# Routed mixture stage: where its rows are scaled, how its front half is ordered, and how lanes are compared

## The reference, cut to what matters

```
logits = x @ gate_w                      # 2048 x 8
top_val, top_id = max(logits), argmax(logits)
score = sigmoid(top_val)
xs = x * score
y[e] = (silu(xs @ rt_gate[e]) * (xs @ rt_up[e])) @ rt_down[e]
routed = y[top_id]                       # one expert for each token
shared = (silu(x @ sh_gate) * (x @ sh_up)) @ sh_down
return shared + routed
```

## Time and profile before

| | |
|---|---|
| median of 3 runs | 928.35 us |
| the profiled execution | 928.58 us, its span 926.8 us |
| mean granted TensorE clock | 0.923 |
| PE, DVE, ACT, POOL busy | 81%, 73%, 40%, 42% |
| first mixture stage | starts near 446.7 us |
| second mixture stage | starts near 812.7 us |
| 23 gathers (L1551), both stages | 43.7 us on POOL |

### The profile page before, as it was taken

How to read it: one execution, slowest core, us unless ns; L and a number is a source line. 1 busy time by engine, 2 the same in 40 slices (tenths; PEclk the granted TensorE clock), 3 DMA queues, 4 the chain that set the end, 5 groups by cost and what they waited for, 6 DMA issues and landing times. The chain is left out here.

```text
span 926.8 us, 16478 instructions
## 1 busy us (share of the span) xinstructions
PE 753.7 (81%) x6055; PEld 497.7 (54%) x6055; DVE 673.2 (73%) x1165; ACT 371.1 (40%) x646; POOL 390.2 (42%) x559
## 2 busy tenths in 40 slices
PE   0578888899989997768874977599999998985693
PEld 0356457788878986346543644244444443553462
DVE  7889777999977799899651338789999995363132
ACT  3113760111116611223411524078888888341151
POOL 3444014888773140355254535223333333126353
PEclk9989898999999999899896989589999999979697
DMA  3000000000000000500112123574000000011113
GB/s 84 0 1 1 1 1 1 1 1 1 1 1 2 1 1 1 171 1 1 40 38 34 39 74 108 164 127 77 10 9 10 10 10 10 7 46 41 28 41 114
DMA packets 33396, 30.28 MB, mean 33 GB/s; under 512 B 6598, under 2 KB 27654, under 8 KB 33318
## 3 DMA queue, kind: packets, MB, share of 16 engines
q1 hardware_dynamic: 29678, 22.37, 9.6%
q0 software_dynamic: 2944, 6.04, 2.7%
q10 hardware_dynamic: 696, 0.82, 0.4%
HBM read 16.89 MB, written 10.35 MB: 29 GB/s over the span
## 5 line engine op out<-in xcount | busy, mean ns | idle before, releaser
L2246 DVE TENSOR_REDUCE blockmax<-c_bank 128x8 f32<-128x1024 f32 x144 | 173.1, 1220 | 21.0 <-PE c_bank L2377 16.6
L2307 ACT ACTIVATE PT<-c_bank 128x1024 f32<-128x1024 f32 x144 | 146.9, 1027 | 36.7 <-PE c_bank L2399 34.4
L2413 PE MATMUL c_bank<-PT,V 128*9 128x256 f32 (+1 forms) x1408 | 87.0, 344 | 3.7 <-ACT OT L2299 2.6
L2370 PE MATMUL c_bank<-KA,QA 48*128 48x128 bf16 (+3 forms) x608 | 60.6, 284 | 23.9 <-DMA KA<-PT 8.8
L2196 POOL TENSOR_SCALAR_AFFINE_SELECT PT<-PT 128x256 f32<-128x256 f32 x128 | 49.1, 407 | 69.8 <-ACT PT L2307 69.8
L1007 PE MATMUL sums<-prod,ident 128*128 128x128 f32 x512 | 67.4, 288 | 9.5 <-DVE prod L1080 8.7
L1007 PEld LDWEIGHTS sums<-prod,ident 128*128 128x128 f32 x512 | 62.0, 198 | 17.0 <-DVE prod L1080 13.4
L1556 POOL DMA_INDIRECT routed_results<-results_m,target_m x46 | 44.5, 968 | 52.3 <-DVE results_m L1812 49.5
L400 PE MATMUL gu_f<-gu_wT,xqT_f 128*128 128x352 f32 x128 | 49.5, 533 | 13.9 <-DVE h_f L320 11.1
L2399 PE MATMUL c_bank<-QA,KA 51*128 51x128 bf16 (+3 forms) x480 | 57.1, 301 | 0.7 <-DVE blockmax L2246 0.7
L1835 DVE TENSOR_TENSOR r_h_m<-r_silu_m,m_bank_m 128x256 f32<-128x256 f32 x46 | 19.3, 421 | 52.2 <-ACT r_silu_m L1735 52.2
(11 more groups left out here) (379 smaller groups left out, 1773.4 us busy)
## 6 DMA issues: line engine op xcount, KB each, us to landing
scaled_rows<-xs_m SPq DMA_DIRECT2D x8, 256.0 KB, 2.2
back_m<-routed_results SPq DMA_DIRECT2D x8, 256.0 KB, 3.7
qk_parts_dram<-PT SPq DMA_DIRECT2D x8, 256.0 KB, 2.7
qk_parts_dram<-PT SPq DMA_DIRECT2D x4, 384.0 KB, 3.5
QA<-qk_parts_dram SPq DMA_DIRECT2D x6, 256.0 KB, 4.5
KA<-qk_parts_dram SPq DMA_DIRECT2D x6, 256.0 KB, 6.5
m_gu<-in_rt_gate SPq DMA_DIRECT2D x1, 1024.0 KB, 5.8
m_gu<-in_rt_up SPq DMA_DIRECT2D x1, 1024.0 KB, 8.3
```

Of the source, the lines that this page charges most:

```text
L2246: nc.vector.tensor_reduce(blockmax[:, h % 2, :, HALFQ * n:HALFQ * (n + 1)], slot_of((1, m)).rearrange("p b (n c) -> p b n c", c=P), AX.X, ...
L2307: nc.scalar.activation(PT[:, u % PRING, :, :], slot_of((0, u)), ACT.Exp, scale=SCALE).then_inc(s_pt, 1)
L2370: ins = nc.tensor.matmul(out[:, b, n * P:end * P], QA[at, h, PLACE[i] * P:(PLACE[i] + 1) * P], KA[at, h, spot * P:(spot + end - n) * P], s ...
L2413: ins = nc.tensor.matmul(O[32 * g:32 * g + DH + 1, f * P:f * P + n], V[:, b, j, h, :], PT[:, u % PRING, b, o:o + n], start=(a % len(VALUES ...
```

## The change

- GpSimd no longer scales rows. ScalarE does it after its second shared silu, in 16 activations of 128x128 with the score as per-partition scale; the semaphore now counts tiles, and SyncE waits for four a quarter.
- On TensorE, the logits of chunk 0 stand ahead of the first shared product, those of chunk 1 between the transposes of chunks 2 and 3; both products of the shared half 1 stand ahead of the counting instead of one on each side of it.
- On VectorE both shared_hidden of chunk 0 stand ahead of sorted_place; before, the second one stood behind it.
- in_lane is made by 16 tensor_scalar instructions, one for each tile, whose one scalar is that tile's lane per partition, and the 0..127 row is bf16, not f32. The semaphore is still raised once every four tiles.

```diff
-        self.lane = k.sb("m_lane", [P, P], ctx=ctx)
+        self.lane = k.sb("m_lane", [P, P], BF16, ctx=ctx)
...
-                    sp.wait_ge(s_xs, g + 1)
+                    sp.wait_ge(s_xs, GROUP * (g + 1))
...
-                pool.wait_ge(s_score, 1)
-                pool.wait_ge(ln.s_xn, TILES)
-                for g in range(NB):
-                    at = slice(GROUP * g, GROUP * (g + 1))
-                    nc.gpsimd.tensor_tensor(xs[:, at, :], ln.xn[:, at, :], wide(score[:, at], [P, GROUP, D]), ALU.mult).then_inc(s_xs, 1)
...
-                pe.wait_ge(s_xnT, 1)
+                route(0)
                 shared_product(0, 0, 0)
                 turn(2)
-                pe.wait_ge(s_xnT, 2)
+                route(1)
+                turn(3)
                 shared_product(0, 0, 1).then_inc(s_sgu, 1)
-                turn(3)
-                for g in range(NB):
-                    route(g)
-                shared_product(0, 1, 0)
+                route(2)
+                route(3)
+                shared_gate_up(0, 1)
                 count()
-                shared_product(0, 1, 1).then_inc(s_sgu, 1)
...
                 shared_act(1)
+                act.wait_ge(s_score, 1)
+                for t in range(TILES):
+                    nc.scalar.activation(xs[:, t, :], ln.xn[:, t, :], ACT.Identity, scale=score[:, t:t + 1]).then_inc(s_xs, 1)
                 shared_act(2)
...
-                    for g in range(NB):
-                        at = slice(GROUP * g, GROUP * (g + 1))
-                        nc.vector.tensor_tensor(in_lane[:, at, :], wide(low[:, at], [P, GROUP, P]),
-                                                moe.lane[:, :].unsqueeze(1).to_broadcast([P, GROUP, P]), ALU.is_equal).then_inc(s_lane, 1)
+                    for t in range(TILES):
+                        ins = nc.vector.tensor_scalar(in_lane[:, t, :], moe.lane[:, :], low[:, t:t + 1], None, ALU.is_equal)
+                        if t % GROUP == GROUP - 1:
+                            ins.then_inc(s_lane, 1)
...
-                shared_hidden(0)
+                for n in range(HALVES):
+                    shared_hidden(n)
                 sorted_place()
-                shared_hidden(1)
                 slot_and_lane()
```

## The result

The changed kernel took 920.43 us (median of 11 runs, 916.2 to 925.0), the kernel before 927.18 (11 runs, 924.26 to 928.64): ratio 0.9929 [0.9911, 0.9947], a gain of 6.75 us where 3.6 was forecast.

The account below looks back on a forecast made before the run. The start of the gathers was taken to bound each mixture stage, with TensorE's results held back a fixed time behind it. With the clock kept, 1.15 plus 2.45 gave 3.6 us: 928.35 to 924.8, range 922.6 to 929.6.

Parts of the forecast that it names:

- the front: Work ahead of the first gather in each mixture stage: 1.15 us gained in the first, 2.45 in the second, together 3.6.
- The gathers' start: In each mixture stage, when the gathers may begin was the number that counts; the loop was assumed to follow one for one.
- falls as before: Rival: TensorE's clock falls in both stages' fronts as it did; sum +0.7 us, 929.0; chance 0.27.
- falls earlier: Rival: TensorE's clock falls ahead of the last logits, +2.1 and +1.5 us in the stages, 932.0; chance 0.15.
- the lanes: VectorE's 16 in_lane compares: 3.65 us with the collision, 0.6 us slower a stage; bounds 1.3 to 4.8.
- The term per tile: Duration of one VectorE lane compare of 128 bf16 columns with one scalar: 251 ns at best.
- the collision: A VectorE lane compare lengthened by GpSimd's half of number starting then: 0.62 us a stage.
- the step from start to start: Time between starts of successive VectorE lane compares: 173 to 207 ns a tile, 2.8 to 3.4 us for 16.
- where clock changes fall in the loop adds about 1 us either way: In the slot loop, shifting TensorE clock changes were given about 1 us either way, beside the summed gain of 3.6.
- The low end of the range, 922.6: The fastest total forecast, for lanes 1.1 us a stage cheaper than taken.
- it ends at a fixed distance behind the first gather: What holds TensorE's results back ends some 32.6 us behind each stage's first gather, where the loop's first silu runs.

Follow-up runs that it names:

- gps_scale: The changed kernel with the scaling of rows given back to GpSimd; 888.44 us, 0.9990 of the kernel before.
- before_again: The kernel before, unchanged, run once more for a profile on another chip; 887.48 us, ratio 0.9991.
- load_late: The changed kernel with TensorE's first two reads of expert numbers moved behind the last shared projection; 920.81 us, 0.9934 of the kernel before.
- gather_split: The changed kernel with 12 gathers ahead of the slot loop and the others each behind a scatter; 900.6 us, 1.0155 of the kernel before.
- after_third: The changed kernel, unchanged, run a third time on another chip; 926.78 us, 1.0013 of the kernel before.
- warm_late: The changed kernel with dummy TensorE products around its lanes wait and the first two expert-number reads behind the last shared projection; 922.55 us, 0.9977 of the kernel before.
- warm_old_lanes: The changed kernel with dummy TensorE products around token_numbers and the four broadcast compares; 923.49 us, 0.9972 of the kernel before.
- sets 1 and 2: The changed kernel again, its parts undone, and tests of what starts the loop; on these chips the kernel before took 888.13 and 887.54 us.
- set 3: Both kernels and two undone parts, with TensorE made to wait for the last gathered rows; the unmodified kernel before took 889.12 us.
- set 4: Old-lane variants of the changed kernel and the changed kernel itself, on a slower chip; the kernel before took 925.89 us.
- warm_front: The changed kernel with dummy TensorE products around its wait for the lanes; 884.23 us, 0.9965 of the kernel before.
- old_routes: The changed kernel with the logits in one block behind the transposes, as before; 888.92 us, 0.9992 of the kernel before.

## Why the prediction was right, and where not

The time came out 4.4 us below the 924.8 forecast. Of this 1.2 is the starting point: the forecast counts down from 928.35, and the kernel before took 927.18 in the comparison. The other 3.15 is gain that the sum didn't have. Of the 7.8 us between the profiles, the front has 0.9 more than forecast, the loop 3.2, D 0.15; about 1 us of that doesn't show between the medians.

**Right: the front.** The gathers' start was the number to count in the comparison, and where TensorE was made to wait for the last of them. It moved by 1.56 and 2.91 us against 1.15 and 2.45 forecast, and in every profile of the changed kernel it lies 20.6 to 20.8 us behind the first tile, whatever the chip (22.3 to 23.5 before). GpSimd's multiplication beside VectorE was the cause of the long products: 1156 and 772 ns became 291 and 376, and were long again in `gps_scale`. The clock lasted through the front, so count ran early and sorted_place started 11.68 us behind the first tile in both stages (12.89 and 13.52 before). Of the rivals, "falls as before" happened in no profile of the changed kernel; "falls earlier" was seen once, in `gps_scale`, where the gather came 3.3 us later than in that profile's other stage.

**Mis-sized: the lanes.** Taken at 3.65, they took 3.29. The term per tile was nearly exact (243 ns against 251), and so was the collision (0.61 against 0.62); what was off was the step from start to start: 3.29 less 0.61 over 16 is 168 ns, below the 173 to 207 of the prediction, which took the middle. This is 0.36 in each stage, 0.7 of the 0.9 that the front's sum fell short; the rest is within a few tenths of its other terms. The old lanes took 3.10, and with them the first gather is 0.1 to 0.3 us earlier: by themselves the scalar compares gave nothing. By the formula of the Trainium skill ("VectorE: DVE Perf Modes", section on the TRN2 errata) 16 tiles would take 1.5 us, an estimate; the trace disagrees, with 2.68 without the collision. The same section of the Trainium skill says that the formula is too low for single operations and puts their measured fixed part at about 150 cycles of 0.96 GHz, which is an estimated 156 ns, and the rows' 160 agrees. By its advice, tiles of at least 512 elements, the old form is the better one, and the rows agree by that small margin. The sharing that the Trainium skill states ("GPSIMD Engine Reference", Specifications) is borne out: one compare that ran while GpSimd made its half of number took 854 ns against 243.

**Failed: "where clock changes fall in the loop adds about 1 us either way".** This term was mis-sized, and it held most of the missing time. The loops were 1.72 and 1.44 us shorter, 3.16 in sum, where the sum had nothing for them and "about 1" beside it. The low end of the range, 922.6, was made of cheaper lanes alone. Before, the clock was at its lower level until some 5 us into each loop; after, its low stretches lie ahead of the loop, where results from TensorE come late anyway and the lower clock costs nothing. That the level is the cause, and not the change, is shown by `before_again`, whose loops begin at the upper level without the change and take 40.17 and 39.99 us (after 40.13 and 40.95, before 41.85 and 42.39), and by the two stages of `load_late`. In all profiles but that of `gather_split`, loops with at most 0.3 us at the lower level took 39.95 to 40.95 us, and those that began with 4.5 to 6.9 us of it took 41.5 to 42.6. Why the second loop of after took 40.95 at the upper level is open. That the low stretches ended ahead of both loops was foreseen by nothing in the prediction, and this part of the gain counts as luck. Both loops of `after_third` began with no more than 0.2 us of it as well, but the second loop of `load_late` began low behind the same front, and so did both loops of `warm_late` and `warm_old_lanes`.

**Failed as a general claim: "it ends at a fixed distance behind the first gather".** In this comparison it held (32.55, 32.61). But it is a property of the chip that ran. On the chips of sets 1 and 2 it was 13.8 to 17.8; then the loop's start is the end of TensorE's own chain, and the low stretch behind the lanes, free in the comparison, now costs what the front gained. The result is 0.998. (On the chip of set 3, where the kernel before was as fast, no kernel was profiled without the wait put in by hand.) On that of set 4 it was 35.2 and 35.3, since the last shared silu stood at 28.4 and its remainder no longer fitted under the gathers. That takes back some 5 us of the gain; the ratio of 1.001 rests on executions that have no profile. The gain of 0.7% is therefore shown for the chip of the comparison alone, and the earlier gathers, 1.6 to 2.9 us a stage, for all.

**Open.** What holds TensorE's results back while the gathers run, and only on some chips. Shown: the 39 us between the two kinds of chip (926 and 888) all lie in the two mixture stages, which are 19.4 and 20.7 us longer (96.84 against 77.48, 98.56 against 77.85); 35.6 of it lies between first gather and first silu, the rest in the loops. TensorE's work isn't what is late: in the kernel before its first gate and up products of the loop are recorded from 491.45 to 493.33, and the silu that needs them starts at 503.64. The waits are "remote"; it ends about 4 us behind the end of the last gather's issue; it isn't the read of expert numbers. Why executions of `after_third` fall in two groups wasn't found either, nor why its last shared silu was caught later than that of the comparison (28.4 against 23.3 behind the gather), though the kernel is the same.

**The better version** depends on the chip for the same reason. `warm_front` was the fastest where nothing is held back (884.23, against 887.54 for before beside it; the changed kernel had 887.77 in another set). `warm_old_lanes` was, where the changed kernel gained nothing (923.49 against 926.78 on one chip). Neither is shown to beat the changed kernel on the chip of the comparison.

## What to carry to other kernels

Ask of every gain in a front what binds behind it, and test that by moving the suspect both ways: delaying the gathers showed in one run that they didn't bind there. A stage that waits for something "remote" at a fixed distance may not do so on the next chip, so repeat a comparison on another one before trusting a gain under 1%. When a clock dip moves, follow it to its new place: under a wait for something else it costs nothing, in the chain that binds it takes back what was won.

## What the runs showed of the hardware

- The same kernel took about 888 us on three chips and 926 on two others, and 927 on that of the comparison (which chip that was isn't on record). In one profile of each kind 40.1 of the 40.7 us between them lie in the two stages with 23 indirect gathers each.
- VectorE's products of two SBUF tiles of 128x128 take 291 ns alone and up to 1156 beside GpSimd's multiplication. A one-scalar compare of 128 bf16 columns takes 243 alone and took 854 once when it met one.
- Sixteen such compares (168 ns from start to start) are no cheaper than four 512-column compares with broadcast operands (680 ns each).
- TensorE kept its upper clock level through 11.8 us with thin matmuls of the router among transposes and dense products, and lost it near the end of one block of them (`old_routes`, at 454.6 and 802.9). It also lost it at the lanes, behind waits of 0.89, 0.30 and 0.38 us between short pieces; three dummy products there kept it (`warm_front`).
- A slot loop of some 40 us is 1.5 to 2.5 us longer when the granted clock is at its lower level for its first 4.5 to 6.9 us.
